# Scores and side results in one rotation of three PSUM banks, row maxima over 1024 columns, and all residual tiles read beside the expert blocks

## What is computed

```
x = x + scale(x) * groupnorm(x)               # a small gate per image and channel, scale from DCT sums
t = tokens of x                               # 1024 tokens of 128
t = t + attn(layernorm(t))                    # 8 heads of 16
    q, k, v, t4 = split(z @ W_qkv)
    out1 = softmax(q k^T / 4) v
    out2 = softmax(-|i - j| / e) t4           # fixed decay, done as two scans
    out  = concat(out1, out2) @ W_out + b
t = t + moe(layernorm(t))                     # 8 experts, the best 2 per token
    y = sum over the two of gate * (relu(z w1 + b1) w2 + b2)
out = t back in the image's layout
```

## Time and profile before

| | us |
|---|---|
| median of 3 runs | 2376.35 |
| lowest, highest | 2370.98, 2392.26 |
| the profiled execution | 2371.68 |
| its span, first to last instruction | 2369.9 |
| busy: PE, DVE, ACT, POOL | 2076.4, 1897.7, 1460.3, 1019.7 |

### The profile page before, as it was taken

The page is one execution under the profiler, slowest core; times in us unless marked ns, Lnnn a source line. Parts: engine busy times, 40 slices in busy tenths (PEclk is TensorE's granted clock), DMA queues, the critical chain, the costliest instruction groups (busy, mean ns, idle before and its releaser), DMA issues.

```text
span 2369.9 us, 35246 instructions
## 1 busy us (share of the span) xinstructions
PE 2076.4 (88%) x11552; PEld 962.0 (41%) x11552; DVE 1897.7 (80%) x3669; ACT 1460.3 (62%) x2897; POOL 1019.7 (43%) x1479
## 2 busy tenths in 40 slices
PE   2699999999999999999999999999999378777743
PEld 1233343433333343334334333333433156666633
DVE  5768799999999999999999999999881366676732
ACT  1127777777777777777787777777674134344410
POOL 2101224444342444434344443433333646777764
PEclk9999999999999999999999999999995688999965
DMA  5330322323132222313222232312012277666659
GB/s 172 55 50 1 55 46 47 91 38 79 29 76 46 47 53 40 76 29 78 46 47 52 41 73 34 77 37 47 15 51 84 77 234 257 205 204 209 209 186 339
DMA packets 100990, 215.06 MB, mean 91 GB/s; under 512 B 30224, under 2 KB 50392, under 8 KB 100376
## 3 DMA queue, kind: packets, MB, share of 16 engines
q1 hardware_dynamic: 78000, 166.96, 28.7%
q0 software_dynamic: 17280, 35.95, 4.3%
q10 hardware_dynamic: 5528, 9.91, 1.2%
HBM read 104.30 MB, written 61.23 MB: 70 GB/s over the span
## 4 chain that ended last, share of the span: by engine, by line
PE 59%; DVE 16%; POOL 8%; DMA 6%; issue 5%; ACT 4%; SPq 1%; ACTq 1%; POOLq 0%; DVEq 0%
PE ps L881 22%; PE ps L893 18%; DVE row_max L1420 11%; POOL y_dram L767 7%; PE ps L860 3%; PE ps L837 2%; ACT region L1170 2%; DMA y_dram<-region 2%; DMA big<-w_dram 2%; DMA region<-y_dram 2%; DVE region L1471 2%; PE ps L845 2%; PE ps L849 2%; PE ps L912 1%; PE ps L925 1%
## 5 line engine op out<-in xcount | busy, mean ns | idle before, releaser
L1420 DVE TENSOR_REDUCE row_max<-ps 128x1 f32<-128x512 f32 x2048 | 1292.3, 680 | 133.4 <-PE ps L860 117.0
L1170 ACT ACTIVATE region<-ps 128x512 f32<-128x512 f32 x2048 | 1093.5, 602 | 377.6 <-PE ps L881 373.0
L860 PE MATMUL ps<-big 48*128 48x512 f32 x2048 | 836.8, 479 | 32.6 <-DMA big<-k_parts 14.7
L881 PE MATMUL ps<-big 50*128 50x512 f32 x2048 | 781.2, 463 | 25.9 <-ACT region L1170 15.0
L881 PEld LDWEIGHTS ps<-big 50*128 50x128 f32 x2048 | 325.9, 191 | 655.9 <-ACT region L1170 505.2
L893 PE MATMUL ps<-region 128*32 128x512 f32 x4096 | 569.7, 629 | 0.0
L860 PEld LDWEIGHTS ps<-big 48*128 48x128 f32 x2048 | 346.3, 193 | 131.8 <-DVE row_max L1420 100.1
L767 POOL DMA_INDIRECT y_dram<-region x284 | 272.0, 958 | 120.0 <-issue 82.6
L713 POOL DMA_INDIRECT xs_dram<-region,slot x256 | 249.2, 974 | 81.2 <-issue 71.8
L649 POOL TENSOR_TENSOR norm_v<-norm 128x8 f32<-128x8 f32 x32 | 6.7, 210 | 573.4 <-DVE norm L1409 573.4
L1021 PE MATMUL ps<-big 128*128 128x512 f32 x284 | 125.9, 443 | 73.2 <-DMA big<-w_dram 72.7
(11 more groups left out here) (183 smaller groups left out, 2032.1 us busy)
## 6 DMA issues: line engine op xcount, KB each, us to landing
big<-w_dram SPq DMA_DIRECT2D x71, 514.0 KB, 4.6
big<-q_parts SPq DMA_DIRECT2D x384, 64.0 KB, 2.4
big<-k_parts SPq DMA_DIRECT2D x372, 64.0 KB, 2.4
region<-xs_dram SPq DMA_DIRECT2D x71, 264.0 KB, 2.9
region<-y_dram SPq DMA_DIRECT2D x16, 1024.0 KB, 10.0
region<-in_x SPq DMA_DIRECT2D x28, 512.0 KB, 5.2
t_dram<-region SPq DMA_DIRECT2D x16, 512.0 KB, 3.4
out<-region ACTq DMA_DIRECT2D x16, 512.0 KB, 6.0
```

The costliest lines, as they stand in the source:

```text
L860: pe.matmul(ps[:, M_BANK + half % M_BANKS, :], lane_rows(q_stack[k % 2], h, SHIFT_ROW)[:, t * P:(t + 1) * P], lane_rows(k_stack[k % 2], h, ...
L881: pe.matmul(ps[:, E_BANK + score % E_BANKS, :], lane_rows(k_stack[k % 2], h, STACK)[:, t * P:(t + 1) * P], lane_rows(q_stack[k % 2], h, ST ...
L1170: act.activation(probs[:, u % 2, step_head(k, s, i), :], ps[:, E_BANK + score % E_BANKS, :], ACT.Exp, scale=DH ** -0.5).then_inc(exp_done, 1)
L1420: dve.tensor_reduce(row_max[:, c, h * TILES + t:h * TILES + t + 1], ps[:, M_BANK + half % M_BANKS, :], AX.X, ALU.max).then_inc(max_done, 1)
```

## The change

1. Scores and sides share a ring of the banks 0, 1 and 7 (RING). `ring_order` lists scores and sides in PE's order and gives each the next bank of the three; who takes a bank waits for the copy-out of what was in it: a score (`exp_done`) or a side (`side_free`). A side still waits also for all earlier sides (`take_side`).
2. The maxima get banks 2 to 5, two pairs. A unit's two halves fill a pair, one reduction takes both (1024 columns), and unit n waits for unit n - 2. The join of the halves is gone; `row_max` has one column per unit.
3. The turned maxima of the second group move from step 27 to 25, the second q from step 25 to 27 (AT_MAX1, AT_PREP).
4. There are 16 residual tiles, 11 in the freed region and 5 in the former stacks, all read beside the blocks (8 to 23). The result is written into the residual tile itself, for the last five images into the first five tiles, once these are stored.

```diff
-AT_MAX1, AT_MAX1_FIRST = 27, 23
+AT_MAX1, AT_MAX1_FIRST = 25, 23
-AT_PREP = ((1, 3), (15, 17), (23, 25), (33, 35))
+AT_PREP = ((1, 3), (15, 17), (23, 27), (33, 35))
...
+RING = (0, 1, 7)
+def ring_order():
+    order, bank, side_after, score_after, ring, early = {}, {}, {}, [], [], 0
+    def take(entry):
+        ring.append(entry)
+        return RING[(len(ring) - 1) % len(RING)], ring[-1 - len(RING)] if len(ring) > len(RING) else ("side", None)
...
+        steps += [(s, "", it, i) for s in range(STEPS) for i in range(HALVES)]
+        for s, kind, j, part in sorted(steps):
+            if kind == "":
+                if 0 <= it * STEPS + s + 1 < IMAGES * STEPS:
+                    early = early or len(order)
+                    at, (of, last) = take(("score", len(score_after)))
+                    score_after.append((at, of, early - 1 if last is None else last))
+            elif 0 <= j < IMAGES:
+                key = (kind, j, part)
+                bank[key], side_after[key] = take(("side", len(order))) if score_after else (RING[-1], ("side", None))
+                order[key] = len(order)
+    return order, bank, side_after, score_after
...
-        result = [part(TOK) for _ in range(C_BUFS)]
-        T2_BUFS = 12
-        t2_in = [big_part(TOK).bitcast(F32) for _ in range(5)] + [part(TOK) for _ in range(T2_BUFS - 5)]
+        IN_BIG = 5
+        t2_in = [part(TOK) for _ in range(IMAGES - IN_BIG)] + [big_part(TOK).bitcast(F32) for _ in range(IN_BIG)]
+        result = t2_in[0:IMAGES - IN_BIG] + t2_in[0:IN_BIG]
-        E_BANK, M_BANK, O_BANK, SIDE_BANK = 0, 3, 6, 7
-        E_BANKS, M_BANKS = 3, 3
+        M_BANK, O_BANK = 2, 6
...
-                if T2_FROM <= b < T2_FROM + T2_BUFS:
+                if T2_FROM <= b < T2_FROM + IMAGES:
...
-                if C_BUFS <= k < C_BUFS + IMAGES - T2_BUFS:
-                    sp.wait_ge(result_done, k - C_BUFS + 1)
-                    sp.dma_start(t2_in[k - C_BUFS], t2_dram[k - C_BUFS + T2_BUFS]).then_inc(t2_late, 16)
...
+            def take_side(*key):
+                pe.wait_ge(side_free, side_at[key])
+                kind, last = side_after.get(key, ("side", None))
+                if kind == "score":
+                    pe.wait_ge(exp_done, last + 1)
...
-                half = HALVES * unit + c
-                if half >= M_BANKS:
-                    pe.wait_ge(max_done, half - M_BANKS + 1)
-                pe.matmul(ps[:, M_BANK + half % M_BANKS, :],
...
+                if unit >= 2:
+                    pe.wait_ge(max_done, unit - 1)
+                mm = pe.matmul(ps[:, M_BANK + 2 * (n % 2) + c, :],
...
+                if c == HALVES - 1:
+                    mm.then_inc(full_ready, 1)
...
-                pe.wait_ge(max_joined, GROUPS * k + g + 1)
-                pe.wait_ge(side_free, side_at["max", k, g])
+                pe.wait_ge(max_done, k * STEPS + (g + 1) * GROUP_ROWS)
+                take_side("max", k, g)
...
-                score = 2 * (k * STEPS + s) + i
-                if score >= E_BANKS:
-                    pe.wait_ge(exp_done, score - E_BANKS + 1)
+                bank, kind, last = score_after[2 * (k * STEPS + s) + i]
+                if kind == "score":
+                    pe.wait_ge(exp_done, last + 1)
+                else:
+                    pe.wait_ge(side_free, last + 1)
...
-                for c in range(HALVES):
-                    half = HALVES * (k * STEPS + n) + c
-                    dve.wait_ge(full_ready, half + 1)
-                    dve.tensor_reduce(row_max[:, c, h * TILES + t:h * TILES + t + 1], ps[:, M_BANK + half % M_BANKS, :],
-                                      AX.X, ALU.max).then_inc(max_done, 1)
-                if (n + 1) % GROUP_ROWS == 0:
-                    rows = slice(n + 1 - GROUP_ROWS, n + 1)
-                    dve.wait_ge(max_done, HALVES * (k * STEPS + n + 1))
-                    dve.tensor_tensor(row_max[:, 0, rows], row_max[:, 0, rows], row_max[:, 1, rows],
-                                      ALU.max).then_inc(max_joined, 1)
+                dve.wait_ge(full_ready, k * STEPS + n + 1)
+                at = M_BANK + 2 * (n % 2)
+                dve.tensor_reduce(row_max[:, h * TILES + t:h * TILES + t + 1], ps[:, at:at + 2, :], AX.XY,
+                                  ALU.max).then_inc(max_done, 1)
...
-            dve.wait_ge(t2_in_done, T2_BUFS * 16)
+            dve.wait_ge(t2_in_done, IMAGES * 16)
...
-                if k >= C_BUFS:
-                    dve.wait_ge(stored[k % C_BUFS], (k // C_BUFS) * 16)
-                if k == T2_BUFS:
-                    dve.wait_ge(t2_late, (IMAGES - T2_BUFS) * 16)
-                dve.tensor_tensor(result[k % C_BUFS], t2_in[k % T2_BUFS],
+                if k >= IMAGES - IN_BIG:
+                    dve.wait_ge(stored[k - (IMAGES - IN_BIG)], 16)
+                dve.tensor_tensor(result[k], t2_in[k],
```

More of the change, by code:

```diff
@@ L133, in side_order @@
     for key in first:
-        order[key] = len(order)
+        bank[key], order[key] = RING[-1], len(order)
     for it in range(-1, IMAGES + 1):
@@ L453, in build @@
         t2_in_done = sem("t2_in_done")
-        t2_late = sem("t2_late")
-        stored = [sem(f"stored{n}") for n in range(C_BUFS)]
+        stored = [sem(f"stored{n}") for n in range(IN_BIG)]
+        stored_late = sem("stored_late")
         consts = [(ident[:, :], "ident"), (group_mean, "group_mean"), (wt_t, "wt_t"), (wo2, "wo2"),
@@ L848, in values_and_z @@
                     c = b - HALVES
-                    pe.matmul(side, wvz[:, P:2 * P], norm_ch[k % 2][:, c * BANK:(c + 1) * BANK], start=True,
+                    pe.matmul(side("vz", k, b), wvz[:, P:2 * P], norm_ch[k % 2][:, c * BANK:(c + 1) * BANK], start=True,
                               stop=True).then_inc(side_ready, 1)
@@ L1156, in t2_out @@
                 act.wait_ge(side_ready, side_at["turn_t2", k, c] + 1)
[L1157 removed]
+                act.activation(n2_row[:, 4 * c:4 * c + 4, 0:P], side_tiles("turn_t2", k, c), ACT.Copy).then_inc(side_free, 1)
             def exp_gap(k):
@@ L1267, in _ @@
                 act.wait_ge(result_done, k + 1)
-                act.dma_start(out[k], result[k % C_BUFS]).then_inc(stored[k % C_BUFS], 16)
-            for n in range(C_BUFS):
-                act.wait_ge(stored[n], ((IMAGES - 1 - n) // C_BUFS + 1) * 16)
+                act.dma_start(out[k], result[k]).then_inc(stored[k] if k < IN_BIG else stored_late, 16)
+            for n in range(IN_BIG):
+                act.wait_ge(stored[n], 16)
+            act.wait_ge(stored_late, (IMAGES - IN_BIG) * 16)
         @block.vector
```

113 lines of the change are left out of this document (53 added, 60 removed).

## The result

The changed kernel takes 2401.43 us (median of 17 runs, 2392.98 to 2413.53), the kernel before 2370.98 in the same comparison (17 runs): ratio 1.0126, 95% interval 1.0104 to 1.0148, slower by 30 us. The forecast was 16 to 21 slower, so the sign and the range held; the size did not, and it is over the 1% that the forecast stayed under.

The account below looks back on a forecast made before the run. PE and DVE both full early in an image, DVE bounding the scans, PE the rest. Fourteen images at 3.75 - 1.07 - 1.2 = 1.48 give +20.7, the end -4.8: +16 on 2376.35, 2392 us; range 2345 to 2418.

Parts of the forecast that it names:

- The ring's wait: Scores behind a side on PE wait for the exponential two back: 0.24 per four-transpose side, 3.75 us an image.
- Ten sides and three shorter ones: Per image, ten of twelve four-transpose sides paid, 2.4 us; shorter sides: turned maxima twice, 0.9, and dispatch, 0.45.
- The relief: Wide maxima on DVE give back 1.07 us an image in the scan stretch and 1.2 outside it.
- clear idle time outside them: Sign that the forecast is right: DVE clearly idle outside the scan stretch.
- The spacing of 1.13: One 1024-column reduction on DVE holds it 1.13 us to its follower, saving 0.067 per unit.
- the choice of the row: Back-to-back 512-column reductions on DVE, 1.20 for two, taken as the basis instead of the skill's 125 ns a unit.
- The moved steps: Turned maxima moved from step 27 to 25 and second q from 25 to 27: costs nothing.
- Images 1 to 14: Fourteen middle images each pay 3.75 - 1.07 - 1.2 = 1.48 us, +20.7 us together.
- The step that failed: First and last image, 0 and 15: ring cost and relief both counted at nothing.
- Image 0: First image: PE waits for DVE, so relief and ring cover each other; counted at nothing.
- The clock rival: PE's new waits bring a fall to half clock in every image: 12 us more, 2404 us; chance 0.07.
- The end: Closing loop without four residual reads: 5.6 us less; reads beside blocks 20 to 23 cost 0.8; together -4.8 us.

Follow-up runs that it names:

- ring3_halves: Changed kernel with its maxima put back to halves of 512 columns in banks 3 to 5, joined in pairs, bank 2 empty; 2415.31 us, ratio 1.0184 to before.
- after_two: Changed kernel with each wide maximum replaced by two of 512 columns over the same pair of banks, join back; 2415.98 us, ratio 1.0175 to before.
- after_late_bias_filler: Changed kernel, last image: ACT's weight copies in sixteen pieces, one-column matmuls moved to step 62, extra 48-row matmul beside each score; 2412.74 us, ratio 1.0188 to before.
- the filler run: Changed kernel with one more 48-row matmul beside each score of the last image from step 24 on; 2408.73 us, ratio 1.0151 to before.
- experiments 4, 5 and 7 to 10: Changed kernel with: 4 moved steps put back, 2401.40 us; 5 after_two; 7 the filler run; 8 last-image weight copies in sixteen pieces, 2387.51 us; 9 after_late_bias; 10 after_late_bias_filler.
- after_late_bias: Changed kernel, last image: ACT's weight copies in sixteen pieces and the 32 one-column matmuls moved from step 38 to 62; 2391.88 us, ratio 1.0073 to before.

## Why the prediction was right in direction and too small

- **The ring's wait.** The mechanism and its price per side were right to a hundredth: 0.34 to 0.48, and 0.43 behind it; 512-column sides cost nothing. The sum was too large: 3.75 forecast, 1.84 measured by the pair with three and four banks. Ten sides and three shorter ones were taken as paid; nine steps show it, and part comes back in the next steps.
- **The relief.** 2.27 forecast (1.07 in the scans, 1.2 outside). The image has grown by 1.11 (104.44 against 103.33) with a ring that costs 1.84, so the relief is 0.73, if the ring costs the same with either kind of maxima. The 1.35 between `ring3_halves` and the changed kernel are more, since they also hold what the moved steps cost with halves (0.57 by 103.95 against 103.38), which the kernel before does not pay. The scans gave back 0.5; by `after_two` the wide instruction's own part is 0.33 an image. DVE does have clear idle time outside them, as the forecast said, and PE does not use it. The spacing of 1.13 was right, and so was the choice of the row: 1.20 less 1.13 is 0.07 a unit. The fixed cost of a PSUM-sourced instruction in the Trainium skill (VectorE: DVE Perf Modes, "The TRN2 errata"), 120 cycles, would make it 0.125, an estimate from that figure; back to back, half of that does not show.
- **The moved steps** cost nothing, as forecast, but with maxima in four banks only: with three the same moves cost 13 us.
- **Images 1 to 14.** Two terms too large by much the same (1.91 and 1.54), so the net was near, which is luck: 1.48 an image forecast, 1.1 at the full clock, 0.95 with the falls, 13.4 us in place of 20.7. The other five kernels with this code up to image 14 took 1470.0 to 1480.2 for the fourteen, 11 to 21 more than the kernel before.
- **The step that failed**: "Image 0 does one and a half units a step, so PE waits for DVE there and relief and ring cover each other; image 15 has no F beyond step 24. I count both at nothing." The last image lost 11.4, and not to the ring's waits by themselves: 0.9 up to step 48, and 10.5 behind it, at half clock where the kernel before is at the full one. `ring3_halves`, with the same ring and its clock back, takes 112.8 there. What the sum lacked is a term for the clock in the image whose last forty steps have no F, where the kernel before too spends 54.6 of 114.3 us at the half level. A fourth bank there brings the clock back and gives more than the image had lost.
- **Image 0** and the units ahead of it lost 4.2 together. The units ahead gained 5.2: they end at 136.9 to 137.4 in all kernels with wide maxima, at 141.7 to 142.5 with halves in three banks. Image 0 lost 9.4. The profile's record of the clock begins at its first change, at 186.7 before and at 181.1 after; up to there PEclk reads 1.00, but the values take what they take at half clock, 1.93, in both kernels. Such values, and the stretch behind it, before, then after:

```profile
178.72 1.93 PE L893 MATMUL ps<-region 128*32 128x512 f32 x8
...
186.70:269.70 83.00, 73.24 (x444) 27.58 (x444) 69.77 (x136) 61.58 (x117) 17.12 (x30) 0.99 0.13 21
...
178.14 1.93 PE L916 MATMUL ps<-region 128*32 128x512 f32 x8
...
181.10:273.90 92.80, 81.28 (x448) 29.80 (x444) 67.97 (x87) 63.11 (x118) 17.01 (x30) 0.89 0.11 19
```

The second stretch is 9.8 longer and holds two falls, from 194.7 to 204.9 and from 222.0 to 232.3. The same code with the clock up from 176.6 on and one fall of 3.4 before the last step (`after_late_bias_filler`) does image 0 in 129.0. So this part of the loss goes with the clock and not with a term of the forecast. The other six kernels with maxima in pairs of banks took 133.8 to 140.7 there, those with halves in three banks 125.8 to 129.2, so it may well belong to the change; why is open.
- **The clock rival** came nearer to the time, 2404, than the forecast, but by another way: not a fall in every image (in the profiled execution ten of the images 2 to 14 have none or 3.4 us of it), but one that does not end in the last. The Trainium skill's section on psum-queue depth-cycling (TensorE: Matmul & The Clock Gate, "A second HAM failure mode: psum-queue depth-cycling") lays falls to small pauses of PE between groups. The row of the filler run, 84.20 busy of 84.20 at 0.50, speaks against pauses as what keeps it down here.
- **The end**: -5.6 forecast, -5.1 measured in the closing loop. The 5.1 more from the last score to the last send (0.8 forecast) are not explained by the four reads.

Open: why the clock does not come back in the last image of the kernels that have three banks in the ring and their maxima in pairs of banks. All seven profiled (the changed one, experiments 4, 5 and 7 to 10; in 5 the reductions are not wide) kept it down until some 1941 to 1956 (one of them with 6.8 us up), while `ring3_halves`, with the same ring and the same matmuls there, had it back after 41 us in all, and the kernel before after 54.6 with the same pace of steps, 4.13. Behind the last score the others are at half clock again for most of that time, the kernel before from 1849.0 to 1910.4. With one profile of each kernel, chance is not excluded for any one of them.

## What to carry to other kernels

Before a bank is taken from a rotation, count how many entries lie between a score and the next use of its bank, with every guest in it, and lay that on the delay of the engine that empties it; a guest costs the entries behind it even if it is emptied early. Do that for each phase by itself, the last repetition above all, where a stream that had covered the delay is gone: there a rotation can be longer, since the stream's banks are free. In the kernel here that was worth 31 us. And a gain on an engine that shares the bound is worth what the other engine lets through: of 55 us less DVE work, images 1 to 14 saw 10 (14 x 0.73).

## What the runs showed that was not expected

- PE busy without a pause, 84.20 of 84.20 us, stayed at half its granted clock; without the filler and with one more bank for the scores PE was back at the full clock after 13.6 us, busy 12.31 of 13.60.
- Where the clock falls in the middle images it does so at one place, behind the 8-column logits: all falls in images 1 to 13 of the changed kernel begin between the first scores of steps 31 and 32.
- How often the clock falls is not set by the code alone: the same attention code had a fall in seven of the images 1 to 14 in one execution (the changed kernel) and in thirteen in another (`after_late_bias`).
- In these traces PEclk reads 1.00 before the first change on record, whatever the clock is. The duration of a known matmul tells the level: eight values take 1.93 at half clock and 1.06 at the full one.
